# The first half of each expert tile's down product in three F32R products instead of one float32 product, with the parts made by GpSimd, ScalarE and VectorE

## The reference

```
g = jnp.einsum('th,ehi->tei', xt, Wg)
u = jnp.einsum('th,ehi->tei', xt, Wu)
y = jnp.einsum('tei,eih->teh', jax.nn.silu(g) * u, Wd)
routed = jnp.einsum('tke,tk,teh->th', oh, w, y)
shared = jax.nn.silu(xt @ sWg) * (xt @ sWu) @ sWd
return (routed + shared).reshape(b, s, h)
```

## Time and profile before

| | |
|---|---|
| median of 3 runs | 966.77 us (966.26 to 967.22) |
| the profiled execution, own time | 964.48 us |
| its span, first to last instruction | 962.7 us |
| mean granted TensorE clock | 0.988 of full |
| TensorE busy | 899.1 us, 93% of the span |
| VectorE, ScalarE, GpSimd busy | 658.3, 604.0, 439.7 us |
| down products of the tiles (L1654) | 188 records, 88.4 us busy |

### The profile page before, as it was taken

One profiled execution on the slowest core, in us unless ns is written; L12 is line 12 of the kernel. 1 busy time (PEld: TensorE's weight loads), 2 busy tenths in 40 slices (PEclk: granted clock), 3 DMA queues, 4 the chain that ended last, 5 costly groups with the idle time before them and its releaser, 6 DMA issues.

```text
span 962.7 us, 21706 instructions
## 1 busy us (share of the span) xinstructions
PE 899.1 (93%) x6859; PEld 684.3 (71%) x6859; DVE 658.3 (68%) x1657; ACT 604.0 (63%) x1318; POOL 439.7 (46%) x486
## 2 busy tenths in 40 slices
PE   6778899999999999999997899999999999999995
PEld 5335678787887978878785677767776776776673
DVE  8886567576666757666675767868877666666662
ACT  6323577776777777777787833331157777777773
POOL 9276553533515346251500415633344577356332
PEclk9799999999999999999999999999999999999998
DMA  6135442324324242332313521271459478736530
GB/s 232 42 101 139 131 115 57 97 57 102 98 56 100 49 118 68 81 97 52 98 44 92 216 89 77 80 282 55 177 177 388 146 138 188 258 61 129 61 44 1
DMA packets 60514, 110.53 MB, mean 115 GB/s; under 512 B 15412, under 2 KB 21556, under 8 KB 58098
## 3 DMA queue, kind: packets, MB, share of 16 engines
q1 hardware_dynamic: 48082, 87.15, 29.1%
q0 software_dynamic: 12320, 21.99, 12.0%
HBM read 53.03 MB, written 25.17 MB: 81 GB/s over the span
## 4 chain that ended last, share of the span: by engine, by line
PE 73%; SPq 8%; DVE 7%; issue 5%; ACT 2%; POOL 2%; DMA 1%; ACTq 0%; POOLq 0%; DVEq 0%
PE psum L1576 13%; PE psum L705 10%; SPq L451 8%; PE psum L1654 8%; PE psum L718 6%; PE psum L695 6%; PE psum L661 5%; PE psum L648 5%; PE psum L670 5%; PE psum L1495 3%; PE psum L1608 2%; PE psum L1598 2%; PE psum L627 1%; PE psum L1587 1%; PE psum L721 1%
## 5 line engine op out<-in xcount | busy, mean ns | idle before, releaser
L792 ACT ACTIVATE probs<-psum,nmax 128x128 f32<-128x128 f32 (+7 forms) x256 | 191.2, 747 | 37.1 <-DVE nmax L834 33.7
L834 DVE CUSTOM_DVE_ANT_0 psum<-psum,mask_row 128x128 f32<-128x128 f32 (+7 forms) x256 | 192.1, 766 | 26.6 <-PE psum L695 25.1
L705 PE MATMUL psum<-ident,probs 128*128 128x128 f32 x1152 | 174.6, 276 | 13.0 <-ACT probs L792 6.1
L705 PEld LDWEIGHTS psum<-ident,probs 128*128 128x128 f32 x1152 | 134.1, 140 | 48.6 <-ACT probs L792 18.3
L777 ACT COPY probsT<-psum 128x512 f32<-128x512 f32 (+3 forms) x256 | 129.2, 505 | 33.2 <-PE psum L705 30.5
L1068 POOL DMA_INDIRECT out<-xnT,slot_out x47 | 81.4, 1732 | 100.8 <-DMA out<-xnT,slot_out 68.5
L488 POOL CAST part_hi<-full 128x512 fp32r<-128x512 f32 x28 | 17.1, 610 | 206.1 <-ACT full L565 160.3
L695 PE MATMUL psum<-k_low,q_stack 128*128 128x512 f32 (+2 forms) x256 | 104.3, 415 | 6.2 <-ACT probs L792 2.6
L849 DVE TENSOR_TENSOR attnT<-psum,z_rows 128x128 f32<-128x128 f32 x64 | 18.6, 291 | 111.3 <-ACT z_rows L799 111.3
L1654 PE MATMUL psum<-w_dn,gated_T 128*128 x188 | 88.4, 593 | 1.0 <-ACT gated_T L1131 1.0
L1418 DVE TENSOR_TENSOR w_lo<-w_gu,w_hi 128x1024 fp32r<-128x1024 f32 x48 | 58.7, 1225 | 40.4 <-ACT w_hi L1160 39.4
(11 more groups left out here) (280 smaller groups left out, 2134.2 us busy)
## 6 DMA issues: line engine op xcount, KB each, us to landing
w_gu<-in_wgu SPq DMA_DIRECT2D x16, 1024.0 KB, 6.7
q_stack<-part_hi SPq DMA_DIRECT2D x128, 64.0 KB, 2.0
q_stack<-part_lo SPq DMA_DIRECT2D x128, 64.0 KB, 2.0
w_dn<-in_wd SPq DMA_DIRECT2D x16, 512.0 KB, 8.6
out<-acc SPq DMA_DIRECT2D x17, 256.0 KB, 3.6
hot_all<-xn SPq DMA_DIRECT2D x4, 1024.0 KB, 8.6
h_scratch<-hot_all SPq DMA_DIRECT2D x16, 256.0 KB
k_low<-part_hi SPq DMA_DIRECT2D x64, 64.0 KB, 2.0
```

What stands on the lines that cost most here:

```text
L705: mm = pe.transpose(bank(4 + m % 2)[:, (j - 4 * k) * P:(j - 4 * k + 1) * P], probs[n % PSLOTS][:, j * P:(j + 1) * P], ident[:, :])
L792: act.activation(probs[n % PSLOTS][:, 0:(i + 1) * P], score_bank(n)[:, 0:(i + 1) * P], ACT.Exp, bias=nmax[:, n % 4:n % 4 + 1], scale=-1.0, ...
L834: dve.tensor_tensor_reduce(out=row, in0=row, in1=mask_row[:, (QT - 1 - i) * P:QT * P], scale=1.0, scalar=3.0e38, op0=ALU.add, op1=ALU.min, ...
```

## The change

The two down parts in `ws_hi` and `ws_lo` (blocks KC and KC+1), which held the split down weights of the shared expert and are not used after it, become two pairs of buffers, `dn_hi[0..1]` and `dn_lo[0..1]`. For every tile the first 128 inner channels of the down product go through them:

- GpSimd makes the high part of the weights (`down_high(j)`), one 128x512 cast. `down_high(0)` and `down_high(1)` stand behind the gathers 0 to 13; in turn j `down_high(j + 2)` stands between `gather(j + 14)` and `add(j)`. It waits until the down product of tile j, the last user of the buffer, is done.
- VectorE makes the low part (`down_low(j)`, 128x512) behind `row_low(j + 2)`, and the low part of the turned activations (`gated_low(j-1)`, 128x128) at the head of turn j. The latter is what now releases the down product.
- ScalarE's one copy of the turned rows, 128x256, becomes a 128x128 cast into `gs_hi` and a 128x128 copy into `gated_T`.
- TensorE does three F32R products for the first half, one float32 product for the second. It waits for `gated_low` and `down_low` of the tile.

```
 def moe_pool:
+            def down_high(j):
+                if j > LAST:
+                    return
+                e = pool.value_load(tile_e_i[0:1, j:j + 1], min_val=0, max_val=E - 1)
+                slot = pool.snap(e % WRING)
+                pool.wait_ge(s_whi, 2 * j + 1)
+                pool.wait_ge(s_y, SHARED + max(j - 1, 0))
+                pool.tensor_copy(dn_hi[j % 2], w_dn[:, bass.ds(slot, 1), 0, :].rearrange("p o n -> p (o n)")
+                                 ).then_inc(s_dnhi, 1)
...
             for j in range(X_RING // 2, GATHER_AHEAD):
                 gather(j)
             for j in range(TILES):
+                if j == 0:
+                    pool.wait_ge(s_plan, EXPERTS_PLANNED)
+                    down_high(0)
+                    down_high(1)
                 if j + GATHER_AHEAD < TILES:
                     gather(j + GATHER_AHEAD)
+                down_high(j + 2)
                 add(j)
...
 def moe_act: turn_copy(n, p)
-                act.copy(gated_T[:, p, :], bank(4 + p)[:, 0:FF]).then_inc(s_gC, 1)
+                act.copy(gs_hi[:, p, 0:P], bank(4 + p)[:, 0:P]).then_inc(s_gshi, 1)
+                act.copy(gated_T[:, p, P:FF], bank(4 + p)[:, P:FF]).then_inc(s_gshi, 1)
...
 def moe_dve:
+            def down_low(j):
+                e = dve.value_load(tile_e_i[0:1, j:j + 1], min_val=0, max_val=E - 1)
+                slot = dve.snap(e % WRING)
+                dve.wait_ge(s_dnhi, j + 1)
+                dve.tensor_tensor(dn_lo[j % 2], w_dn[:, bass.ds(slot, 1), 0, :].rearrange("p o n -> p (o n)"),
+                                  dn_hi[j % 2].bitcast(F32), ALU.subtract).then_inc(s_dnlo, 1)
+            def gated_low(j):
+                dve.wait_ge(s_gshi, SHARED + 2 * j + 2)
+                dve.tensor_tensor(gs_lo[:, j % 2, 0:P], bank(4 + j % 2)[:, 0:P], gs_hi[:, j % 2, 0:P].bitcast(F32),
+                                  ALU.subtract).then_inc(s_gC, 1)
...
             for j in range(TILES):
+                if j >= 1:
+                    gated_low(j - 1)
                 weight_low(j + 1, 1)
                 gate(SHARED + j, j % 2)
                 row_low(j + 2)
+                down_low(j)
                 weight_low(j + 2, 0)
...
 def moe_pe: down_of(j, half)
-                for k in range(2):
-                    mm = pe.matmul(bank(6 + p), gated_T[:, p, k * P:(k + 1) * P],
-                                   w_dn[:, bass.ds(half, 1), k, :].rearrange("p o n -> p (o n)"), start=(k == 0),
-                                   stop=(k == 1))
-                mm.then_inc(s_y, 1)
+                pe.wait_ge(s_dnlo, HOT_C + j + 1)
+                for t, (g, w) in enumerate(((gs_hi, dn_hi), (gs_lo, dn_hi), (gs_hi, dn_lo))):
+                    pe.matmul(bank(6 + p), g[:, p, 0:P], w[p], start=(t == 0), stop=False)
+                pe.matmul(bank(6 + p), gated_T[:, p, P:FF],
+                          w_dn[:, bass.ds(half, 1), 1, :].rearrange("p o n -> p (o n)"), start=False,
+                          stop=True).then_inc(s_y, 1)
```

More of the change, by code:

```diff
@@ L270, in build @@
         w_lo = [w_lo0[:, :, :], ws_lo[:, 0:KC, :]]
+        dn_hi = [ws_hi[:, KC + i, :] for i in range(2)]
+        dn_lo = [ws_lo[:, KC + i, :] for i in range(2)]
         s_dve2 = sem("dve_router_step")
@@ L356, in build @@
         s_dve = sem("dve_step")
-        s_act = sem("act_step")
+        s_dnhi = sem("down_weights_high_ready")
         s_ohhi = sem("hot_onehot_hi_ready")
         s_ohlo = sem("hot_onehot_lo_ready")
+        s_dnlo = s_ohlo
         s_row = sem("hot_row_part_ready")
@@ L1483, in moe_dve @@
                     adds_needed()
+            gated_low(LAST)
         def moe_pe(pe):
```

## The result

The changed kernel took 1002.96 us (median of 4 runs, 1002.1 to 1005.28) against 967.0 us (966.26 to 968.9) for the kernel before: a ratio of 1.038, 95% interval 1.0362 to 1.0398. It is slower by 36 us.

The account below looks back on a forecast made before the run. TensorE was taken to bound the kernel. Losses of 15.1 + 2.9 + 16.0 + 0.2 = 34.2 us on the profiled 964.48 gave 998.7, and with the median 2.3 above it 1001 us; range 985 to 1012.

Parts of the forecast that it names:

- The start: Ahead of tile 0's down product: the first cast stands behind gather 13, making the product 15.1 us late.
- The clock and turn 1: Tile 0 to tile 1: first product at half clock, turn of 8.55 us against 5.67, 2.9 more.
- The ring: Steady turns: down product, y_scale, weight_high, weight_low and gated_low wait in a circle of 5.50 us; 43 x 0.37 = 16.0 us.
- TensorE's part: Down product of each tile: 0.17 us less, 8.0 us in all if nothing is waited for.
- The end: Last two turns: one gains 0.17 us, tile 46's chain is bare; in all 0.2 us more.
- register loads of 0.3 become visible: Upper bound of the steady turn, 5.65 us; 6.5 us either way over 43 turns.
- signs of being wrong: Turns of 4.96 us, down_low waiting for GpSimd behind adds, or the first cast before 716.9.
- the rival in which GpSimd becomes the ring: Steady turns: GpSimd's casts stand behind adds waiting for earlier landings; 16 us lost, 1017 us; chance 14%.
- a lag of 4 to 8: GpSimd's adds: expected 6 to 7 us apart against turns of 5.5, falling 4 to 8 behind.
- the blocking rival: Steady turns: GpSimd and VectorE block each other, each cast costing 0.61 us; 26 us more, 1027 us; chance 2%.
- they should miss each other: Steady turns: GpSimd's cast starts right after the down product, weight_low 2.3 us later, so no overlap.
- The signs: Expected profile: 15 us gap before tile 0, first cast near 727.8, clock 0.5, 0.5 us idle per steady product, down_low idle near zero.

Follow-up runs that it names:

- casts_early: Changed kernel with down_high(0) and down_high(1) moved ahead of GpSimd's wait for the output stores and gathers 8 to 13; 999.1 us.
- gated_first: Changed kernel with VectorE's gated_low(j) ahead of weight_low(j+2, 0) instead of behind it; 990.0 us.
- ring_alone: Changed kernel with the down-weight cast on VectorE directly ahead of down_low, none on GpSimd, gated_low still behind weight_low; 985.4 us.
- products_only: Changed kernel without down_high, down_low, gated_low and their waits, ScalarE's copies and TensorE's products kept, output not the reference's; 958.6 us.
- load_first: Changed kernel with the cast on VectorE, and ScalarE loading the expert's number into its register ahead of y_scale's wait; 973.1 us.
- narrow_cast: Changed kernel with gated_low ahead of weight_low and GpSimd casting 64 of 512 columns, output not the reference's; 986.6 us.
- plan_and_load: Changed kernel with the cast on VectorE, gated_low ahead of weight_low, planning steps in the shared expert, register load ahead of y_scale's wait; 959.3 us.

## Why the prediction was right, and which term was missing

The forecast was 1001 us, measured were 1003. Compared with the profiled execution, as the prediction's sum was: 34.2 us forecast, 37.6 found. That the sum is within 3.4 us is in part luck: the forecast terms came out some 4 us smaller in all, and 7.6 us were in no term. By its steps:

**The start.** 15.1 forecast, 14.2 found. The cast ran at 726.79 and not 727.75. It followed gather 13 without the gap of 0.30, and gather 13 itself began at 725.80, 0.66 earlier than before, though the first of the six began 0.9 later: with VectorE standing still each took 1.00 or less, where before three of them took 1.27, 1.77 and 1.54. casts_early showed that the cast's place was the cause of 11.2 of the 14.2 us, by moving tile 0 to 719.90; the other 3.0 stayed.

**The clock and turn 1.** 2.9 forecast, 2.8 found; the first product ran at half clock as priced.

**The ring.** Forecast 5.50 a turn, found 5.43. The links of the ring are in the rows of the turn from tile 1 to tile 2, ScalarE and VectorE after:

```profile
741.41 0.69 ACT L1165 ACTIVATE xnT<-psum,slot_w 128x512 f32<-128x512 f32 x1 [2.03 <-PE psum L1694]
742.26 1.05 ACT L1180 CAST w_hi<-w_gu 128x1024 fp32r x1 [0.16 <-SPq L945]
```

```profile
743.50 1.22 DVE L1438 TENSOR_TENSOR w_lo<-w_gu,w_hi 128x1024 fp32r<-128x1024 f32 x1 [0.69 <-ACT w_hi L1180]
744.65 0.28 DVE L1454 TENSOR_TENSOR gs_lo<-psum,gs_hi 128x128 fp32r<-128x128 f32 x1
```

From the product's start at 739.55 to y_scale 1.86 us (forecast 1.84), to weight_high 0.85 (0.83), to weight_low 1.24 (1.25), to gated_low 1.15 (1.14), its length 0.28 (0.29), and from its end to the product at 744.99 0.06 (0.15). The last link makes the difference. So the ring cost 43 x 0.306 = 13.2 us, not 16.0. gated_first opened it and got turns of 4.98; ring_alone kept it alone and got 5.43. This is shown.

**TensorE's part.** 0.17 a tile forecast, 0.15 found (4.98 against 5.13 in products_only).

**The end.** 0.2 forecast, none found.

**The missing term.** 43 turns lost 20.8 us, of which the ring is 13.2. The other 7.6 us sit in thirteen turns and were in no term of the sum:

- 2.8 us by register loads. In four turns (tiles 9, 13, 33, 36: 0.61 to 0.64 each over the ring) 1.46 to 1.49 us instead of 0.84 lie between y_scale and weight_high, in tile 43's (0.30) 1.14. The prediction had this only as "register loads of 0.3 become visible" in the bounds. Before, ScalarE's idle 0.86 hid it: two of 44 distances were 1.12 and 1.13 there too, and the turns stayed at 5.13. load_first removed this kind.
- 2.2 us by GpSimd at tiles 7, 23 and 24 (0.28, 0.29, 1.67). `down_low` waited 1.24, 1.26 and 2.79 us for the cast. GpSimd and VectorE after, at tile 24:

```profile
862.54 1.60 POOL L1082 DMA_INDIRECT out<-xnT,slot_out  x1 [3.53 <-DMA out<-xnT,slot_out]
864.45 1.05 POOL L1051 DMA_INDIRECT xnT<-xn_scratch,slot_tok  x1 [0.31 <-issue]
865.50 0.62 POOL L1064 CAST ws_hi<-w_dn 128x512 fp32r x1
```

```profile
866.33 0.69 DVE L1448 TENSOR_TENSOR ws_lo<-w_dn,ws_hi 128x512 fp32r<-128x512 f32 x1 [2.79 <-POOL ws_hi L1064]
867.16 1.23 DVE L1438 TENSOR_TENSOR w_lo<-w_gu,w_hi 128x1024 fp32r<-128x1024 f32 x1
```

  The cast stood behind an add that had waited for the landing of the one before. That `down_low` waits for GpSimd behind adds was one of the prediction's own signs of being wrong; it showed at these three tiles. This is the rival in which GpSimd becomes the ring. It priced 16 us; the prediction expected "a lag of 4 to 8" and no loss. That was nearly right, but only because the late start and the ring gave the adds time. With either gone and the cast still on GpSimd, the same wait brought turns of 7 to 10 us.
- 1.5 us by the clock at tile 25. The gap that GpSimd had caused ahead of tile 24's product was enough to lower it. Windows and ScalarE after:

```profile
868.00:870.00 2.00, 1.36 (x3) 1.09 (x4) 2.00 (x5) 0.00 (x0) 1.77 (x1) 0.69 0.02 6
870.00:872.00 2.00, 2.00 (x4) 0.95 (x3) 0.65 (x2) 0.04 (x1) 1.67 (x2) 0.50 0.34 42
```

```profile
871.96 0.69 ACT L1165 ACTIVATE xnT<-psum,slot_w 128x512 f32<-128x512 f32 x1 [4.27 <-PE psum L1694]
```

  y_scale comes 3.32 us after the product's start at 868.64, not 1.86, which is 1.46 of that turn's 1.48. The long turns of casts_early have this in them too: its granted clock was 0.50 in the windows of 746 to 748 and 756 to 758 us, behind each gap.
- 0.8 us by the blocking rival, in the turns of tiles 10, 12 and 32 (0.47, 0.17, 0.17). A cast of 1.45 us (788.58) lay in `weight_low`, which took 1.70 (787.87) instead of 1.22; in the other two `weight_low` took 1.40 and 1.39 beside casts of 0.91 and 0.90. In those two the other `weight_high` had come 1.05 and 1.00 after the copy in the turn before, which pushed VectorE's work onto the cast. VectorE and GpSimd after, at tile 12:

```profile
799.20 1.40 DVE L1438 TENSOR_TENSOR w_lo<-w_gu,w_hi 128x1024 fp32r<-128x1024 f32 x1 [0.15 <-ACT w_hi L1180]
```

```profile
798.60 0.91 POOL L1064 CAST ws_hi<-w_dn 128x512 fp32r x1
```

- 0.4 us at tile 34, between weight_high's start and weight_low's (1.61 instead of 1.25), stay unexplained.

The prediction rested on the cast and weight_low missing each other ("they should miss each other"). That failed: over all tiles the median cast took 982 ns, not 610, and the slowest 1587. The prediction had looked at weight_low alone, which is 1.22 in the rows of before, where GpSimd made no casts beside it. GpSimd's own rows gave a hint: a gather that began inside a weight_low (720.93 to 722.15) took 1.77, against 1.00 and 0.99 for two that began ahead of one. GpSimd before:

```profile
721.25 1.77 POOL L1048 DMA_INDIRECT acc<-xn_scratch,slot_tok  x1 [0.30 <-issue]
```

Hidden under the ring the blocking cost 0.8 us in all; with the ring open it set the turn, at 5.36 (gated_first, narrow_cast).

**The signs.** The gap of TensorE ahead of tile 0 was 12.14 us and not some 15, the first cast ran at 726.79 and not near 727.8, and ahead of a steady product TensorE idled 0.18 and not 0.5. gs_lo ended these gaps and the clock fell to 0.50, as said. VectorE's idle time at `down_low` was not near zero after tile 1: six waits of 0.82 to 2.79 us.

**What the experiments add.** The forecast of 1001 was nearly met because the ring, the largest steady cost, hid most of two others, the adds and the stretched cast. Of the 36.0 us over the kernel before, taking away the late start alone left 33.7, opening the ring alone 24.6, and both with spread gathers 18.7. The version in which no cast stands behind an add, no ring is closed and no planning step lies in a turn kept the 0.15 us a tile in every turn: plan_and_load, 959.3 us, against the 958.6 of the products without any making of parts.

**Open.** Why the same register load, worth some 0.25 us in most turns (0.84 less the 0.59 of load_first), takes 0.6 us more in some was not settled. That the stretching of cast and weight_low comes from a lock on a shared port is the account of the Trainium skill (SBUF — State Buffer, "SBUF: two separate sides"); the runs show the lengths.

## What to carry to other kernels

A new operation can cost what stands ahead of it in its list, not its own length: a cast of 0.61 us on an engine with half its time free cost 11 us at the start, and turns of up to 10 us behind waiting DMAs. Before moving work to an idle engine, ask what that engine waits for, and whether the bound engine ever had to wait for it until now.

When a new wait ties engines together that only ran side by side, add up the links once around. If that sum is longer than the turn, it is the new turn, and slack that used to hide register loads and small stalls is gone. Removing one of several such causes shows the next one, so what a cause costs on the balance is not what its removal gives back: 11.2 us taken off the start gave 2.3 in the end.

## What the runs showed of the hardware that was not expected

- A register load that was invisible under ScalarE's idle time took 0.26 us of every turn in the ring (5.43 against 5.17) and 0.6 more in four of 43 turns.
- A gap of TensorE of 1.85 us can be enough to bring the clock to half: the F32R products behind it stood 0.43 apart (TensorE in the changed kernel, below). It is not always: in gated_first a gap of 3.07 us ended at 859.33, and the granted clock stayed at 1.00 in the windows behind it. What decides between the two was not settled.

```profile
868.64 0.72 PE L1693 MATMUL psum<-ws_hi,gs_hi 128*128 128x512 f32 x1 [1.85 <-DVE gs_lo L1454]
869.16 0.63 PE L1693 MATMUL psum<-ws_hi,gs_lo 128*128 128x512 f32 x1
869.59 0.63 PE L1693 MATMUL psum<-ws_lo,gs_hi 128*128 128x512 f32 x1
```

- The same cast of 128x512 took 0.41 us on VectorE, 0.61 on ScalarE and 0.61 on GpSimd alone, and 1.45 on GpSimd beside VectorE's weight_lows. Of 128x64 it took 0.24 on GpSimd alone and 1.04 beside them.
- The issue of an indirect DMA on GpSimd was longer beside weight_low too: a gather 1.77 us instead of 1.00 (kernel before, 721.25), an add 2.39 instead of 1.60 (gated_first, 809.94).
